# Cross-attention and a routed mixture of experts on one core: routing of the third token group moved forward, its tables moved to GpSimd, scatters without pauses

## The reference, cut to what matters

```python
a = layernorm(x)
Q, K, V = per-head projections of a, ctx, ctx      # 16 heads of 8 -> 64
attn = softmax(Q K^T / 8) over the 16 heads of ONE token
x = x + (attn V) @ Wo + bo
h = layernorm(x)
probs = softmax(h @ router_w)                      # 8 experts
gate, expert = top_k(probs, 2)
y = ((h @ (wv*sv)[e]) * gelu(h @ (w*s)[e])) @ (w1*s1)[e]
x = x + sum over the two experts of gate * y
```

## Time and profile before

| | |
|---|---|
| median of 3 runs | 269.03 us (267.36 to 270.32) |
| time of the profiled execution | 268.95 us |
| its span | 267.2 us |
| TensorE matmul busy | 222.1 us, 83% |
| VectorE busy | 182.3 us, 68% |
| GpSimd busy | 138.1 us, 52% |
| ScalarE busy | 128.3 us, 48% |
| mean granted TensorE clock | 0.945 of full speed |

### The profile page before, as it was taken

How to read it: one execution, slowest core, us unless ns; L and a number is a source line. 1 busy time by engine, 2 the same in 40 slices (tenths; PEclk the granted TensorE clock), 3 DMA queues, 4 the chain that set the end, 5 groups by cost and what they waited for, 6 DMA issues and landing times.

```text
span 267.2 us, 6351 instructions
## 1 busy us (share of the span) xinstructions
PE 222.1 (83%) x1845; PEld 212.6 (80%) x1846; DVE 182.3 (68%) x437; ACT 128.3 (48%) x346; POOL 138.1 (52%) x151
## 2 busy tenths in 40 slices
PE   7997999997999799877997008999999999999600
PEld 7876988997999798757996008999999999999600
DVE  2799598889899999988777201666665656656326
ACT  2433546667765955258853002555555555545000
POOL 6966536644788899707245445363532434234400
PEclk9997999999999999999999955999999999999955
DMA  5999999997001000112101103221211111000068
GB/s 147 299 174 423 308 337 381 377 381 273 21 1 34 30 22 15 45 42 64 32 20 44 39 31 84 62 64 51 62 45 50 42 51 42 29 10 20 8 207 264
DMA packets 25517, 30.93 MB, mean 116 GB/s; under 512 B 2652, under 2 KB 16896, under 8 KB 25362
## 3 DMA queue, kind: packets, MB, share of 16 engines
q1 hardware_dynamic: 21708, 25.28, 30.0%
q0 software_dynamic: 2528, 4.77, 5.8%
q10 hardware_dynamic: 1254, 0.55, 0.8%
HBM read 16.26 MB, written 14.79 MB: 116 GB/s over the span
## 4 chain that ended last, share of the span: by engine, by line
PE 57%; DMA 11%; DVE 10%; issue 7%; POOL 7%; ACT 6%; SPq 1%; POOLq 0%; DVEq 0%; ACTq 0%
PE bank L1009 21%; PE bank L1028 11%; PE bank L887 9%; DMA routed<-rows,pos 7%; PE bank L934 6%; POOL routed L543 3%; ACT w_sb L642 3%; DVE qk L1148 3%; DMA pv<-expert_out 2%; PE bank L942 2%; DVE pv L325 2%; PE bank L896 2%; PE bank L994 1%; PE bank L863 1%; PE bank L945 1%
## 5 line engine op out<-in xcount | busy, mean ns | idle before, releaser
L560 POOL DMA_INDIRECT expert_out<-yo,xs x39 | 39.9, 1023 | 56.3 <-DVE yo L1362 38.7
L325 POOL TENSOR_TENSOR pv<-probs,ctx_sb 128x1408 f32<-128x1408 f32 x14 | 40.2, 2869 | 18.6 <-DVE probs L1202 18.5
L543 POOL DMA_INDIRECT routed<-rows,pos x32 | 35.1, 1098 | 23.5 <-DMA routed<-rows,pos 14.5
L1353 DVE TENSOR_TENSOR hid<-bank,act_sb 128x512 f32<-128x512 f32 x39 | 26.9, 691 | 27.3 <-PE bank L1009 25.0
L1009 PE MATMUL bank<-xsT,g_tile 128*128 128x128 f32 x312 | 42.4, 280 | 3.5 <-DVE g_tile L1344 3.5
L1009 PE MATMUL bank<-xsT,v_tile 128*128 128x128 f32 x312 | 42.1, 279 | 0.0
L1009 PEld LDWEIGHTS bank<-xsT,g_tile 128*128 128x128 f32 x312 | 38.7, 195 | 4.1 <-DVE g_tile L1344 4.1
L1028 PE MATMUL bank<-w_sb,hid 128*128 x312 | 41.9, 278 | 0.0
L1344 DVE TENSOR_TENSOR g_tile<-g_sb,g_scale 128x512 f32 x39 | 27.0, 693 | 18.2 <-PE bank L1009 9.0
L1009 PEld LDWEIGHTS bank<-xsT,v_tile 128*128 128x128 f32 x312 | 38.8, 196 | 0.0
L1028 PEld LDWEIGHTS bank<-w_sb,hid 128*128 128x128 f32 x312 | 38.5, 194 | 0.2 <-issue 0.2
(11 more groups left out here) (178 smaller groups left out, 304.6 us busy)
## 6 DMA issues: line engine op xcount, KB each, us to landing
routed<-pad_rows SPq DMA_DIRECT2D x4, 2080.0 KB, 20.6
xs<-routed SPq DMA_DIRECT2D x39, 65.0 KB, 1.8
g_sb<-in_L_ffn_w_dram SPq DMA_DIRECT2D x1, 2048.0 KB, 11.9
g_scale<-in_L_ffn_s_dram SPq DMA_DIRECT2D x1, 2048.0 KB, 16.5
v_sb<-in_L_ffn_wv_dram SPq DMA_DIRECT2D x1, 2048.0 KB, 28.1
pv<-expert_out SPq DMA_DIRECT2D x3, 512.0 KB, 5.2
x_sb<-in_x_dram SPq DMA_DIRECT2D x4, 256.0 KB, 5.6
ctx_sb<-in_ctx_dram SPq DMA_DIRECT2D x4, 256.0 KB, 6.1
```

The lines of the kernel that those rows point to most:

```text
L325: return eng.tensor_tensor(pv[:, b, g0:g1, :, :], probs[:, b, :, g0:g1].rearrange("p h g -> p g h").unsqueeze(3).to_broadcast([P, many, H, ...
L543: pool.indirect_dma_start(out=routed[:, :], out_offset=bass.IndirectOffsetOnAxis(ap=pos[:, m % TOP, m // TOP:m // TOP + 1], axis=0), in_=r ...
L560: pool.indirect_dma_start(out=expert_out[:, :], out_offset=bass.IndirectOffsetOnAxis(ap=xs_i[:, t % XB, P:P + 1], axis=0), in_=yo[:, t % X ...
L1353: v.tensor_tensor(hid[:, c % 2, :], bank[3 + c % 2][:, :], act_sb[:, c % 2, :], ALU.mult).then_inc(hid_ready, 1)
```

## The change

- In GpSimd's steps the scatters now stand behind the values. `sends` changes a little: group 0's go as 2, 1, 2, 3 in four steps, group 1's as 2 in step 11 and 6 in step 13.
- `scatters` has no pauses at all.
- `early_table` goes to GpSimd, behind step 13. VectorE keeps its first parts (counts to tile ends and the comparison, now in `marks`), right behind the counts in step 12. GpSimd makes the rest: ten small operations, with the sums over experts made by halving. `left_table` goes to GpSimd too (four operations), between the scatters of group 2 and those of group 3.
- On VectorE `choices(NG - 2)` and `positions(NG - 2)` stand ahead of the values of tile 15; on TensorE `places(NG - 2)` ahead of `output_sum(NT - 2)`; ScalarE's parts follow. The first three scatters of group 2 are sent ahead of group 3's `second_rstd`, the other five behind it.
- The statistics of tiles 12 to 15 go to ScalarE, and `fill(1)` is gone.

```diff
-            return {9: 2, 11: 4, 12: G * TOP} if n < EARLY_G - 1 else {9: 2, 10: 3, 11: G * TOP}
+            return {9: 2, 10: 3, 11: 5, 12: G * TOP} if n < EARLY_G - 1 else {9: 2, 11: G * TOP}
...
                     for m in range(first, end):
-                        if n >= EARLY_G and m and m % 2 == 0:
-                            for half in scattered[n]:
-                                pool.wait_ge(half, 16 * (m // 2))
...
+                def table(ins):
+                    done[0] += 1
+                    ins.then_inc(pool_table, 1)
+                    pool.wait_ge(pool_table, done[0])
+                def early_table():
+                    at = slice(0, EARLY)
+                    pool.wait_ge(ends_ready, 1)
+                    table(pool.tensor_scalar(jump[:, :], n_tiles[:, :], -float(P), float(REGION), ALU.mult, ALU.add))
+                    table(pool.tensor_tensor(marks[:, 1, :, :], marks[:, 0, :, :],
+                                             jump[:, :].unsqueeze(1).to_broadcast([P, EARLY, E]), ALU.mult))
+                    for many in (4, 2, 1):
+                        table(pool.tensor_tensor(marks[:, :, :, 0:many], marks[:, :, :, 0:many],
+                                                 marks[:, :, :, many:2 * many], ALU.add))
+                    pool.tensor_scalar(w_off[:, at], marks[:, 0, :, 0], float(E - 1), float(F),
+                                       ALU.min, ALU.mult).then_inc(pool_table, 1)
+                    pool.tensor_scalar(s_off[:, at], marks[:, 0, :, 0], float(E - 1), float(P),
+                                       ALU.min, ALU.mult).then_inc(pool_table, 1)
+                    done[0] += 2
+                    table(pool.tensor_scalar(marks[:, 0, :, 1], tile_no[:, at, 0], float(P), None, ALU.mult))
+                    table(pool.tensor_tensor(marks[:, 1, :, 1], marks[:, 0, :, 1], marks[:, 1, :, 0], ALU.add))
+                    pool.tensor_copy(row_off[:, at], marks[:, 1, :, 1]).then_inc(early_ready, 1)
...
                 for t in STEADY:
                     step(t // G, t % G)
+                early_table()
+                scatters(NG - 2, 0, 3)
                 second_rstd(NG - 1, 0, G - 1, NG)
                 second_rstd(NG - 1, G - 1, G, NG + 1)
-                scatters(NG - 2, 0, G * TOP)
+                scatters(NG - 2, 3, G * TOP)
+                left_table()
                 scatters(NG - 1, 0, G * TOP)
...
+                rows_but_gates(NG - 2)
                 exponentials(NT - 1)
                 residual(NT - 3)
+                second_mean(NT - 3)
+                second_squares(NT - 3)
+                logits_exponentials(NG - 2)
                 z_turned(NT - 2)
-                rows_but_gates(NG - 2)
                 residual(NT - 2)
+                second_mean(NT - 2)
+                gates_in(NG - 2)
+                second_squares(NT - 2)
                 value_weights(0, 0)
-                logits_exponentials(NG - 2)
+                load_gelu()
                 z_turned(NT - 1)
                 rows_turned(0, 0)
                 value_weights(1, 1)
                 residual(NT - 1)
-                load_gelu()
+                second_mean(NT - 1)
+                second_squares(NT - 1)
                 rows_turned(1, 1)
                 gelu(0, 0)
-                gates_in(NG - 2)
...
-                        if t >= G:
-                            fill(1)
...
                 value_sum(NT - 2)
+                places(NG - 2)
                 output_sum(NT - 2)
                 value_sum(NT - 1)
                 turn_rows(0, 0, 0)
                 output_sum(NT - 1)
-                places(NG - 2)
...
                 value_share(NT - 2, 0)
                 maximum(NT - 1)
-                early_table()
+                choices(NG - 2)
                 normalise(NT - 1)
+                positions(NG - 2)
                 value_share(NT - 1, 0, H // 2)
                 value_share(NT - 1, H // 2)
-                choices(NG - 2)
                 gate_weights(0, 0)
-                second_statistics(NT - 3)
-                second_statistics(NT - 2)
-                positions(NG - 2)
-                second_statistics(NT - 1)
                 gate_weights(1, 1)
-                left_table()
```

More of the change, by code:

```diff
@@ L245, in xattn_moe_kernel @@
             sem(n) for n in ("counts_psum", "counts_read", "table_step", "early_ready", "table_ready", "spared"))
+        ends_ready, pool_table, left_ready = sem("ends_ready"), sem("pool_table"), sem("left_ready")
         prefilled = [sem(f"prefilled{g}") for g in range(NG)]
@@ L513, in step @@
                 def step(g, j):
-                    for lag in range(PLACES + 1, PLACES + 1 + G):
-                        if a := group_at(g, j, lag):
-                            to_send = sends(a[0])
-                            if lag in to_send:
-                                scatters(a[0], max([0] + [to_send[m] for m in to_send if m < lag]), to_send[lag])
                     if a := group_at(g, j, NORM):
@@ L530, in step @@
                         values(pool, t, b, 0, POOL_KEYS).then_inc(pv_pool, 1)
+                    for lag in range(PLACES + 1, PLACES + 1 + G):
+                        if a := group_at(g, j, lag):
+                            to_send = sends(a[0])
+                            if lag in to_send:
+                                scatters(a[0], max([0] + [to_send[m] for m in to_send if m < lag]), to_send[lag])
                 def scatters(n, first, end):
@@ L547, in scatters @@
                             bounds_check=last_row).then_inc(scattered[n][m % 2], 16)
+                done = [0]
+                def table(ins):
[19 more added lines that the diff above has]
+                    pool.tensor_copy(row_off[:, at], marks[:, 1, :, 1]).then_inc(early_ready, 1)
@@ new lines, in left_table @@
+                def left_table():
+                    table(pool.tensor_scalar(early_end[:, 1:], tile_end[:, :], float(EARLY), None, ALU.min))
+                    table(pool.tensor_tensor(early[:, 0:E], early_end[:, 1:], early_end[:, 0:E], ALU.subtract))
+                    table(pool.tensor_scalar(jump_left[:, :], early[:, 1:], float(P), float(REGION), ALU.mult, ALU.add))
+                    pool.tensor_scalar(left_no[:, :], tile_no[:, 0:LEFT, 0], early[:, 0:1], None,
+                                       ALU.add).then_inc(left_ready, 1)
@@ L814, in keep_warm @@
                         nc.tensor.matmul(bank[7][:, 0:P], ident[:, :], ident[:, :], start=True, stop=True)
-                def fill(many):
-                    for _ in range(many):
-                        nc.tensor.matmul(bank[0][:, P:2 * P], ident[:, :], ident[:, :], start=True, stop=True)
                 pe.wait_ge(pool_set, 2)
@@ L1338, in gate_weights @@
                     if isinstance(t, int) and t == 0:
+                        dve.wait_ge(early_ready, 1)
                         dve.wait_ge(ld_wg, 16)
@@ L1405, in _ @@
                 gated(3, 3)
-                experts_of(late, LEFT)
+                late_experts()
                 hidden(5, 5)
```

90 lines of the change are left out of this document (32 added, 58 removed).

## The result

The changed kernel takes 267.03 us (median, 265.54 to 270.33) beside 268.89 us of the kernel before (267.01 to 270.65), both over 20 runs. The ratio is 0.9936, 95% interval 0.9915 to 0.9958: a gain of 0.6%, where 5.7% were forecast. The profiled execution took 269.07 us with a span of 267.3, 2.0 us above its own median, so its pieces sum to that.

What follows compares the result with a forecast made beforehand. The prediction took TensorE's wait for tile 9's rows, behind GpSimd's paused scatters, as the bound. From 268.95 us it took 12.8 for tile 9's earlier turn and 2.45 for the clock: 253.7, rounded to 253.6, range 250.5 to 259.5.

Steps and rivals of the forecast that it cites:

- the early tiles' old times: After the hand-over: early expert tiles keep their times, TensorE reaching the turn of tile 9 at 147.4, 1 us either way.
- the early table: Hand-over: ten GpSimd operations take 3.5 us after group 1's scatters end at 112.4; early_ready at 116.0, first products 119.4 to 119.6.
- the draining queue: Rival, scatters of groups 2 and 3: each needs 2.4 us back to back, giving 265.1 us; chance 0.06.
- GpSimd blocking in each: Rival, scatters: limited outstanding scatters make GpSimd wait for each forerunner, 3.4 us each, 277.4 us; chance 0.03.
- Scatters without pauses: GpSimd's scatters: 1.28 us each without pauses, upper bound 1.55, piling up nearly nothing in the DMA queue.
- 5.17 us from the last scatter to the turn of tile 9: Ahead of tile 9: the time from the last scatter's start to the turn stays 5.17 us.
- this hits nothing: End of attention: GpSimd's table slows VectorE's last value products by at most its own length, without delaying tile 0.
- The slow-table rival: Rival, hand-over: four tensor_scalars at 1.04 us make all 3.0 us later, plus 2.45 for the clock, 259.1 us; chance 0.13.
- The clock: TensorE ahead of tile 9: a hole of 1.77 us leaves the clock at full, gaining 2.45 us.
- Fills and earlier routing: Attention: twelve fills at 0.22 us, 2.6 us, gain eaten by GpSimd; group 2's earlier routing worth 1.3 us and a margin.
- The scatters go unpaused, yet TensorE waits elsewhere: Rival at tile 9: group 3's counts and tables would delay it, if late tables came 5 us later; chance 0.02.
- Faster by over 1%: Whole kernel: chance 0.96 of a gain over 1%, 2.7 us, even with the queue draining one scatter at a time.

Runs made afterwards that it cites:

- b_no_pause: The kernel before with only the pauses between pairs of scatters of groups 2 and 3 removed: 268.34 us, ratio 0.9971.
- c_vtable_256: The changed kernel with its early table on VectorE and a 256-element GpSimd memset between scatters of groups 2 and 3: 259.32 us, ratio 0.9589 to before.
- a_delay: The changed kernel with a 640-element GpSimd memset between scatters of groups 2 and 3: 265.75 us, ratio 0.9837 to before.
- b_delay: The kernel before without pauses, with a 640-element GpSimd memset between scatters of groups 2 and 3: 264.63 us, ratio 0.9857.
- a_fill: The changed kernel with the unread filling matmul of the attention steps put back: 268.08 us, ratio 0.9956 to before.
- c_vtable_32: The changed kernel with its early table on VectorE and a 32-element GpSimd memset between scatters of groups 2 and 3: 256.88 us, ratio 0.9583 to before.
- c_g3_free: The changed kernel with its early table on VectorE and 256-element memsets between group 2's scatters alone, group 3 unpaused: 257.27 us, ratio 0.9575 to before.
- a_layout: The changed kernel with every buffer at its old address: 268.69 us, ratio 0.9968 to before.
- a_vtable: The changed kernel with its early table back on VectorE, same ten operations: 261.96 us, ratio 0.9725 to before.
- b_window2: The kernel before with each scatter of groups 2 and 3 waiting only for the one two before it, replacing pair pauses: 267.99 us, ratio 0.9959.

## Why the prediction was wrong

The forecast put the turn of tile 10 at 148.8 + 2.9 = 151.7 in the profiled execution; it was at 166.88. The 15.2 us fall into two steps of the prediction, the early tiles' old times (11.4) and the early table (3.9).

**"I keep the early tiles at their old times"** failed. From the first products to group 3's gates before were 133.81 - 119.30 = 14.5 us; after, from first products to the first scatter, 144.30 - 123.35 = 20.9, so 6.4 us more. b_no_pause has 22.0 there and c_vtable_256, spaced, 14.9. Not all 6.4 are stall: to the gates alone it is 14.5 us before, 20.1 after and 14.8 in a_delay, which has the change and no stalls. So 5.3 are the stall, 0.3 the rest, and 0.9 lie from the gates to the first scatter, where the forecast had 0.3. From the first scatter of group 3 to turn 10 the forecast had 151.7 - 134.1 = 17.6; the trace has 22.6, another 5.0: TensorE does not reach tile 9 at 147.4 but stands still ahead of tile 7 until 156.30, and goes on at half clock. Some 10 of these 11.4 us are the stalls (5.3 and 5.0). I had looked for what a longer run of scatters does to the DMA queue (the draining queue, GpSimd blocking in each) and never for what it does to other engines. My witness, the five scatters in a row of group 1, was no control for this: those ran at 1.55 us with VectorE's value products beside them, as slow as c_vtable_256's, and ahead of the expert tiles.

**"Scatters without pauses", 1.28 us each**, was right (1.28), and so was **5.17 us from the last scatter to the turn of tile 9**, where rows are what is awaited: 4.9 (b_delay) to 5.7 (c_vtable_256) in nine traces. The 0.5 us for scatters beside g_tile products did not show: the eighth started 9.10 us after the first, where the forecast had 9.0 + 0.5.

**The early table on GpSimd** was mis-sized in two terms. The ten operations took 5.14 us and not 3.5, and the six scatters ahead of them ended 1.1 us later than the 112.4 forecast (the table began at 113.55). Neither came from where I placed the bound: the tensor_scalars take 0.20 to 0.31 us. Two operations of 72 elements took 1.30 and 1.21 us beside VectorE's values, where a_fill has 0.33 for the first of them, and a scatter took 3.00. I had counted what VectorE loses alone ("this hits nothing") and took from GpSimd's values (2.86 us in either case) that GpSimd doesn't lose; its short operations do. From the table's end to the first products were 4.65 us and not 3.5; 1.0 of the 1.15 more lies behind the turn of tile 0, where the matmuls ran at half clock. So 1.1 + 1.6 + 1.2: first products at 123.35, 3.9 us after 119.5. One trace against another of the same order varies by up to 2.6 us here (note under the table), but all five with this table are later than all with the other. That is the rest of the 15.2 us. The slow-table rival had this consequence, half clock included, from another cause.

**The clock.** Its 2.45 us were to be gained. Instead TensorE's clock was at half for 10.2, 6.8 and 6.9 us around the three holes (116.3 to 126.5, 133.4 to 140.2, 153.8 to 160.7). c_vtable_32 shows the step right where the holes are gone: 2.96 us from the turn of tile 9 to that of tile 10, 2.9 forecast.

**Fills and earlier routing.** Twelve fills at 0.22 us was right (2.4 against 2.6 us), and so was "GpSimd eats the gain" (its values of tile 13 start at 100.39, forecast 100.3). Group 2's routing was ready in time: its first scatter waited for GpSimd alone.

**Rivals.** "The scatters go unpaused, yet TensorE waits elsewhere" was what happened, but I had given it 0.02 with the late tables as its place; in the changed kernel these end at 158.5 because VectorE is stuck behind the same stall. Faster by over 1% had 0.96 since every case shared the untested step. With the table back on VectorE and the scatters spaced, the mechanism comes near what was forecast, some small stalls remaining: c_vtable_32 has its last scatter at 145.29 (forecast 143.6), tile 9 turned at 150.67 (148.8), and 256.88 us (253.6).

**What stays open** is the cause of the stall. Shown is that ScalarE and VectorE go on late behind work of TensorE that its records show as finished, that it takes closely spaced scatters (1.28 us yes, 1.40 little, 1.59 and 1.91 no), that a single run of eight is enough (runs of four give 2.4 to 3.6 us), and that the late stall ends near the run's end: 0.1 us before the eighth scatter's issue is over (c_g3_free), 0.2 to 0.3 us behind the first output after it (changed kernel, a_layout, a_fill, a_vtable), or 1.7 us behind that (b_no_pause). The early one can end in mid-run (b_no_pause). A wait for instructions is not it: in the changed kernel the queues that load instructions moved no packet from 147 to 156 us, and the scatters and the output, all that moved then, kept the DMA engines busy for 15.9% of the time. Whether TensorE's signal is held back, or TensorE itself is later than its records say, the traces can't tell; nor was tried whether scatters of fewer rows do it.

## What to carry to other kernels

Taking a wait out of GpSimd's queue changes how dense its indirect DMAs are, and in this kernel that stalled engines that have nothing to do with them: look, after such a change, for waits with no releaser in the profile beside the runs, and try a small gap between the DMAs before putting the pauses back. A short chain on GpSimd must be costed beside what VectorE runs at that moment and not by the same operations in a quiet stretch; if it gates the next stage, keep it on VectorE. And when all cases of a forecast share one step ("the others keep their times"), that step needs a rival of its own.

## What the hardware showed that I had not expected

- **Dense indirect DMAs of GpSimd stall the engines that follow TensorE.** 1.28 us apart: ScalarE waits 8.66 us (changed kernel), 10.15 (b_no_pause) and 7.12 (c_g3_free) for a turn that TensorE's records show done in 0.27 us. 1.59 us apart: none above 2.7 us until the hole ahead of tile 9, and the kernel before has one of 2.66 there too. The number under way does not decide: with at most two allowed (b_window2) it is 10.15 us again. The mechanism is not known.
- **GpSimd's operations and DMA issues stretch beside a VectorE operation with two SBUF inputs.** The same operation of 72 elements took 0.33 us (a_fill) and 1.30 (changed kernel), one of 36 elements 0.26 (changed kernel) and 1.12 (a_fill), and a scatter's 0.97 us became 3.00. The small operations ended 0.1 to 0.2 us after VectorE's product, the scatter 0.86. The Trainium skill, GPSIMD Engine Reference, section 8 Key points, says that the two engines share SBUF interfaces and contend when VectorE has two SBUF inputs; the trace agrees, and adds that the scatters' issue suffers too.
- **The time of the whole kernel was one landmark plus a constant** (turn of tile 10 plus 102.0 to 102.7 us, in all seventeen traces), whatever went on ahead of it.
